# Late expert tiles of a transformer step: 30 whole tiles of 128 rows become 22 whole ones and 5 that two experts share

## The reference

```python
scores = softmax(x @ gate_w.T)                      # 2048 rows, 8 experts
topk_ids, topk_w = _grouped_topk(scores)            # 2 experts for each row, weights sum to 1
gu = jnp.einsum('th,eih->tei', x, w13_weight)       # 256 -> 2 x 512 for each expert
gate, up = (gu[..., :INTER], gu[..., INTER:])
act = jax.nn.silu(gate) * up * combine[:, :, None]
out = jnp.einsum('tei,ehi->th', act, w2_weight)     # 512 -> 256, summed over the two experts
x = x + out
```

## Time and profile before

| | |
|---|---|
| time, median of 3 runs | 571.71 us (571.24 to 571.86) |
| profiled execution, its own time | 574.95 us |
| its span in the profile | 573.1 us |
| PE busy | 539.4 us (94%) |
| DVE, ACT, POOL busy | 298.0, 243.1, 168.7 us |

### The profile page before, as it was taken

One profiled execution on the slowest core, in us unless ns is written; L12 is line 12 of the kernel. 1 busy time (PEld: TensorE's weight loads), 2 busy tenths in 40 slices (PEclk: granted clock), 3 DMA queues, 4 the chain that ended last, 5 costly groups with the idle time before them and its releaser, 6 DMA issues.

```text
span 573.1 us, 11007 instructions
## 1 busy us (share of the span) xinstructions
PE 539.4 (94%) x3932; PEld 443.8 (77%) x3933; DVE 298.0 (52%) x875; ACT 243.1 (42%) x560; POOL 168.7 (29%) x152
## 2 busy tenths in 40 slices
PE   6999999999979999999999689999999999999990
PEld 5888868867555677777776578899999999999990
DVE  6676668989354776847688865671111112111110
ACT  1234755453346676887677434222122221222220
POOL 3120000102043232324130042226443535544432
PEclk9799999999989999999999999999999999999996
DMA  9920000000010000300640944977787888877621
GB/s 328 392 99 2 2 0 2 1 1 5 32 37 1 2 2 1 111 2 1 235 170 7 351 137 149 281 215 236 207 258 223 245 240 224 262 219 254 187 32 22
DMA packets 28507, 74.15 MB, mean 129 GB/s; under 512 B 5584, under 2 KB 20176, under 8 KB 23216
## 3 DMA queue, kind: packets, MB, share of 16 engines
q1 hardware_dynamic: 14368, 57.66, 28.1%
q0 software_dynamic: 7488, 10.39, 9.9%
q10 hardware_dynamic: 6608, 5.54, 3.1%
HBM read 62.86 MB, written 10.72 MB: 128 GB/s over the span
## 4 chain that ended last, share of the span: by engine, by line
PE 65%; DMA 12%; DVE 8%; issue 8%; POOL 2%; DVEq 2%; ACT 1%; POOLq 0%; ACTq 0%
PE ps L858 45%; DMA out_x<-arena,row_no 11%; PE ps L862 9%; PE ps L1150 7%; DVE arena L1506 1%; DVE mx L1644 1%; POOL keep L384 1%; PE ps L1011 1%; PE ps L942 1%; DMA arena<-in_x 1%; PE ps L1002 1%; DVE heads_out L1658 1%; POOL var_x L348 1%; PE ps L985 1%; DVE ring L1843 0%
## 5 line engine op out<-in xcount | busy, mean ns | idle before, releaser
L858 PE MATMUL ps<-keep,arena 128*128 128x128 f32 (+2 forms) x976 | 114.7, 274 | 1.1 <-ACT keep L627 1.1
L858 PEld LDWEIGHTS ps<-keep,arena 128*128 128x128 f32 x976 | 112.6, 192 | 2.6 <-ACT keep L627 1.5
L1953 DVE TENSOR_TENSOR keep<-keep,ps 128x512 f32<-128x512 f32 x39 | 26.8, 688 | 137.0 <-PE ps L858 134.3
L392 POOL DMA_INDIRECT out_x<-arena,row_no x39 | 61.5, 1576 | 108.9 <-DMA out_x<-arena,row_no 65.0
L1150 PE MATMUL ps<-arena,keep 128*128 x312 | 74.0, 381 | 1.2 <-issue 0.9
L356 POOL TENSOR_TENSOR ring<-arena,keep 128x512 f32<-128x512 f32 x32 | 33.4, 1044 | 116.0 <-PE ps L858 98.1
L1150 PEld LDWEIGHTS ps<-arena,keep 128*128 128x128 f32 x312 | 56.4, 191 | 7.8 <-issue 1.9
L587 ACT ACTIVATE ring<-ps,mx 128x128 f32<-128x128 f32 x192 | 52.3, 393 | 13.3 <-DVE mx L1644 13.3
L627 ACT COPY keep<-ps 128x256 f32<-128x256 f32 x39 | 14.5, 371 | 96.8 <-PE ps L862 96.8
L858 PE MATMUL ps<-ring,arena 128*32 128x128 f32 (+1 forms) x640 | 52.9, 348 | 0.5 <-ACT ring L594 0.4
L348 POOL TENSOR_TENSOR var_x<-var_x,minus_half 128x4 f32<-128x4 f32 x16 | 17.0, 1064 | 111.2 <-DVE var_x L1500 111.1
(11 more groups left out here) (259 smaller groups left out, 815.3 us busy)
## 6 DMA issues: line engine op xcount, KB each, us to landing
arena<-in_w SPq DMA_DIRECT2D x29, 1024.0 KB, 5.2
w_first<-in_w SPq DMA_DIRECT2D x10, 1024.0 KB, 5.4
arena<-in_w SPq DMA_DIRECT2D x8, 512.0 KB, 7.2
keep<-in_keep SPq DMA_DIRECT2D x1, 3099.0 KB, 21.1
ring<-in_fold SPq DMA_DIRECT2D x1, 2112.0 KB, 12.4
arena<-in_x SPq DMA_DIRECT2D x4, 512.0 KB, 10.4
arena<-in_ctxT SPq DMA_DIRECT2D x4, 512.0 KB, 7.8
out_x<-arena ACTq DMA_DIRECT2D x4, 512.0 KB, 3.4
```

What stands on the lines that cost most here:

```text
L392: pool.indirect_dma_start(out=out_d, out_offset=bass.IndirectOffsetOnAxis(ap=row_no[:, t:t + 1], axis=0), in_=YO[t % DEEP], in_offset=None ...
L858: ins = pe.matmul(out, w, m, start=(k == 0), stop=(k == len(pairs) - 1))
L1953: dve.tensor_tensor(HA[r % 2], HA[r % 2], ps[:, 2 * (r % 2) + 1, :], ALU.mult).then_inc(act_ok, 1)
```

## The change

Late rows now lie in 22 whole tiles (`FULL`) and 5 shared ones (`SPLIT`), 27 in all, so the program has 36 tiles where it had 39. A shared tile holds 64 rows of one expert in its lower half and 64 of another in its upper half. They stand at tiles 12, 17, 22, 27 and 32 (`SPLIT_AT`). For a shared tile:

- SP loads two experts' weights, so there are 41 loads of 1 MB where there were 39. A buffer is counted in loads (`load(t)`), not in tiles.
- `gate_up_split` turns the product round: 64 rows are stationary, in one column strip of the array for each half, and the weights stream through, 512 columns at a time.
- The products then have rows on partitions, so TensorE transposes them (`turn_products`) and ACT copies them back (`products_turned`). `down_split` does the two halves in column strips again. ACT copies the second expert's `w2` beforehand (`second_down`), and scales in two pieces of 64 partitions.
- `add` issues two DMAs, one behind the other: the first of 64 rows, the second of all 128, whose lower 64 point at holes.

The planning on DVE (`late_tiles`) finds whole tiles and half tiles for each expert, with more stages; `hot_late` covers all 16 batches where it covered 8. The loop over late tiles is written out.

```diff
-NT = B * S * NPICK // P + NE - 1
+HALF = P // 2
...
+HALVES = (B * S * NPICK - EARLY * P + NE * (HALF - 1)) // HALF
+SPLIT = NE // 2 + 1
+FULL = -(-(HALVES - 2 * SPLIT) // 2)
+LATE = FULL + SPLIT
+NT = EARLY + LATE
...
+SPLIT_AT = [EARLY + 3 + 5 * i for i in range(SPLIT)]
...
+def slot(t):
+    if t < EARLY:
+        return t
+    return EARLY + FULL + SPLIT_AT.index(t) if is_split(t) else t - sum(u < t for u in SPLIT_AT)
+def load(t):
+    return t + sum(u < t for u in SPLIT_AT)
...
-                if t >= DEEP:
-                    sp.wait_ge(u_ps, t - DEEP + 1)
-                e = sp.value_load(e_id[0:1, t:t + 1], min_val=0, max_val=NE - 1)
-                sp.dma_start(W13[t % DEEP], w13_d[bass.ds(e, 1), :, :].rearrange("e p n -> (e p) n")).then_inc(w13_in[t % DEEP], 16)
-            sp.wait_ge(added, 16 * NT)
+                for half in range(1 + is_split(t)):
+                    n = load(t) + half
+                    if n >= DEEP:
+                        sp.wait_ge(u_ps, tile_of(n - DEEP) + 1)
+                    col = expert_at(t, half)
+                    e = sp.value_load(e_id[0:1, col:col + 1], min_val=0, max_val=NE - 1)
+                    sp.dma_start(W13[n % DEEP], w13_d[bass.ds(e, 1), :, :].rearrange("e p n -> (e p) n")).then_inc(w13_in[n % DEEP], 16)
+            sp.wait_ge(added, 16 * load(NT))
...
             def add(t):
                 pool.wait_ge(y_ok, t + 1)
-                if t:
-                    pool.wait_ge(added, 16 * t)
-                pool.indirect_dma_start(out=out_d, out_offset=bass.IndirectOffsetOnAxis(ap=row_no[:, t:t + 1], axis=0),
-                                        in_=YO[t % DEEP], in_offset=None, compute_op=ALU.add).then_inc(added, 16)
+                for half in range(1 + is_split(t)):
+                    if t:
+                        pool.wait_ge(added, 16 * (load(t) + half))
+                    own = slice(0, HALF if is_split(t) and not half else P)
+                    rows_at = row_upper[:, SPLIT_AT.index(t):SPLIT_AT.index(t) + 1] if half else row_no[own, slot(t):slot(t) + 1]
+                    pool.indirect_dma_start(out=out_d, out_offset=bass.IndirectOffsetOnAxis(ap=rows_at, axis=0),
+                                            in_=YO[t % DEEP][own, :], in_offset=None, compute_op=ALU.add).then_inc(added, 16)
...
+            def second_down(t):
+                if t == SPLIT_AT[0]:
+                    act.wait_ge(e_known, 2)
+                    act.wait_ge(w2_in, 16 * NE)
+                    act.wait_ge(placed, 2)
+                else:
+                    act.wait_ge(y_ps, SPLIT_AT[SPLIT_AT.index(t) - 1] + 1)
+                col = expert_at(t, 1)
+                at = act.value_load(e_id[0:1, col:col + 1], min_val=0, max_val=NE - 1) * W2_N
+                act.copy(split_w2, w2e[:, bass.ds(at, W2_N)]).then_inc(split_w2_in, 1)
...
+                if is_split(r):
+                    for half, out in enumerate((Y_PS[r % 2], bank(FEED)[:, 0:D])):
+                        own = slice(HALF * half, HALF * half + HALF)
+                        ins = act.activation(YO[r % DEEP][own, :], out[own, :], ACT.Copy, scale=row_w[r % DEEP][own, 0:1])
+                    ins.then_inc(y_ok, 1)
+                    return
...
+            def gate_up_split(t):
+                first, second = W13[load(t) % DEEP], W13[(load(t) + 1) % DEEP]
+                lower, upper = slice(0, HALF), slice(HALF, P)
+                for a, b in ((1, 0), (0, 1)):
+                    for k in range(KD):
+                        at, bt = ((2 * k + g) * INTER for g in (a, b))
+                        one = pe.matmul(ps[lower, 2 * (t % 2) + a, :], XIT[t % 2][:, k, lower], first[:, at:at + INTER], start=(k == 0), stop=(k == KD - 1))
+                        two = pe.matmul(ps[upper, 2 * (t % 2) + b, :], XIT[t % 2][:, k, upper], second[:, bt:bt + INTER], start=(k == 0), stop=(k == KD - 1))
+                one.then_inc(g_ps, 1)
+                two.then_inc(u_ps, 1)
+            def turn_products(t):
+                pe.wait_ge(act_ok, t + 1)
+                if t == SPLIT_AT[0]:
+                    pe.wait_ge(routed, 2)
+                for k in range(INTER // P):
+                    ins = turn(bank(FEED)[:, k * P:(k + 1) * P], split_rows[:, k * P:(k + 1) * P])
+                ins.then_inc(ha_ps, 1)
+            def down_split(t):
+                pe.wait_ge(ha, SPLIT_AT.index(t) + 1)
+                pe.wait_ge(split_w2_in, SPLIT_AT.index(t) + 1)
+                lower, upper, last = slice(0, HALF), slice(HALF, P), INTER // P - 1
+                at = pe.value_load(e_id[0:1, slot(t):slot(t) + 1], min_val=0, max_val=NE - 1) * W2_N
+                for k in range(INTER // P):
+                    pe.matmul(Y_PS[t % 2][lower, :], HA[t % 2][:, k * P:k * P + HALF], w2e[:, bass.ds(at + k * D, D)], start=(k == 0), stop=(k == last))
+                    ins = pe.matmul(bank(FEED)[upper, 0:D], HA[t % 2][:, k * P + HALF:k * P + P], split_w2[:, k * D:k * D + D], start=(k == 0), stop=(k == last))
+                ins.then_inc(y_ps, 1)
...
                 turn_in(m, r + 2)
+                if is_split(r):
+                    turn_products(r)
                 gate_up(m, r + 1)
                 down(m, r)
...
+                beyond = work
+                dve.tensor_tensor(beyond, place, p_len.unsqueeze(1).broadcast_to([P, B, NE]), ALU.is_ge)
...
+                dve.tensor_scalar(base, p_end[:, NE - 1:NE], float(FULL), 2.0, ALU.max, ALU.mult)
+                dve.tensor_scalar(half_end[:, 0:NE], p_end, 2.0, None, ALU.mult)
...
+                done = cmp2[:, 0:(LATE + SPLIT) * 2 * NE].rearrange("p (t n) -> p t n", n=2 * NE)
+                dve.tensor_tensor(done, half_end.unsqueeze(1).broadcast_to([P, LATE + SPLIT, 2 * NE]), kept("half_no").unsqueeze(2).broadcast_to([P, LATE + SPLIT, 2 * NE]), ALU.is_le)
+                dve.tensor_tensor(jump, odd_at, half_end[:, 0:NE], ALU.subtract)
...
-                dve.tensor_tensor(hot_late[k], kept("col_no").unsqueeze(1).broadcast_to([P, EB, P]),
-                                  col_at[:, k * B + EB:(k + 1) * B].unsqueeze(2).broadcast_to([P, EB, P]), ALU.is_equal)
+                dve.tensor_tensor(hot_late[k], kept("col_no").unsqueeze(1).broadcast_to([P, B, P]), col_at[:, of_k].unsqueeze(2).broadcast_to([P, B, P]), ALU.is_equal)```

TensorE's list, first before. This is one late step in the loop: the transposes of tile t+2, `gate_up` of t+1 (`w_first` is the first weight buffer), then the first of the four matmuls of `down`.

```order
L862 MATMUL ps<-keep 128x128 x2
L858 MATMUL ps<-keep,w_first 128x128 x16
L1141 ISA
L1141 TENSOR_LOAD e_id
L1141 ISA x2
L1150 ISA
L1150 MATMUL ps<-arena,keep 128x256
```

More of the change, by code:

```diff
@@ L37, with is_split, tile_of, expert_at @@
 NEG = -3.0e38
+SPLIT_AT = [EARLY + 3 + 5 * i for i in range(SPLIT)]
+def is_split(t):
+    return t in SPLIT_AT
+def slot(t):
[4 more added lines that the diff above has]
+    return t + sum(u < t for u in SPLIT_AT)
+def tile_of(n):
+    return next(t for t in range(NT) if load(t) <= n <= load(t) + is_split(t))
+def expert_at(t, half):
+    return NT + SPLIT_AT.index(t) if half else slot(t)
 def columns(parts):
@@ L184, in build @@
         HOT_N = EB * P // 2
[L185 to L186 removed]
+        hot_early, hot_late = ([ring[:, at + 1024 * k:at + 1024 * k + n * P // 2].bitcast(BF16).rearrange("p (b n) -> p b n", b=n) for k in range(NPICK)]
+                               for at, n in ((512, EB), (512, B)))
         one_hot_early = sb("one_hot_early", [P, NPICK * EB, EARLY], BF16)
@@ L256, in build, with tiles_of @@
         XT_PS, Y_PS = ps[:, 4, 0:D], [ps[:, 5 + u, 0:D] for u in range(2)]
[L258 to L267, removed]
+        UP = 256
+        split_w2, split_rows = ring[:, 0:W2_N], ring[:, W2_N:W2_N + INTER]
+        def tiles_of(step):
+            for t in range(EARLY, NT - 2):
+                step(0, t)
         def bank(k):
@@ L845, in _ @@
             turned(0, 10)
-            tiles_of(act, step)
+            tiles_of(step)
             answer(0, NT - 3)
@@ L1131, in gate_up @@
                 pe.wait_ge(xt, t + 1)
-                pe.wait_ge(w13_in[r % DEEP], 16 * (m + r // DEEP + 1))
+                for n in range(load(t), load(t) + 1 + is_split(t)):
+                    pe.wait_ge(w13_in[n % DEEP], 16 * (n // DEEP + 1))
+                if is_split(t):
+                    gate_up_split(t)
+                    return
+                w13 = W13[load(t) % DEEP]
                 for g, done in enumerate((g_ps, u_ps)):
@@ L1148, in down @@
                     pe.wait_ge(y_ok, t - 1)
+                if is_split(t):
+                    down_split(t)
+                    return
                 for k in range(INTER // P):
@@ L1482, in _ @@
             down(0, 8)
-            tiles_of(pe, step)
+            tiles_of(step)
             gate_up(0, NT - 1)
@@ new lines, in late_tiles @@
+                dve.tensor_scalar(jump, jump, float(HALF), None, ALU.mult)
+                settle()
```

(8 more changed lines are left out.)

91 lines of the change are left out of this document (59 added, 32 removed).

## The result

The changed kernel takes 599.07 us (median of 4 runs, 596.35 to 610.59), the kernel before 571.79 in the same set: a ratio of 1.044 with an interval of 1.039 to 1.049. Runs more than 1.5% above the fastest of the same kernel (here 610.59) count for a median and not for a ratio. The forecast was 582.5 with a range of 565 to 590. The sign came out as written, and so did the line that sets the end; the size did not: +27 us instead of +11, outside the range.

A forecast was written before the change was run, and what follows sets the result against it. Two serial lines, TensorE and the output adds held by weight loads, were taken to matter, the adds setting the end: +11.0 + 2.3 - 2.5 = +10.8 us on 571.71 gives 582.5 us, range 565 to 590.

The forecast's parts named there:

- Which line ends the kernel: Late stage: the adds set the end, falling about 4 us behind TensorE per shared tile; TensorE waits for gathered rows.
- Strips overlap: Split products on TensorE: two column strips run side by side, `gate_up_split` 3.7 to 3.9 us, `down_split` 1.84.
- rival of 588 us by serial strips: Strips don't overlap at 512 columns: 26 us more on TensorE, 588 us; chance 0.05.
- TensorE by itself: TensorE's side: -16.6 for three tiles fewer, +3.8 for shared tiles, +3.1 for planning, -9.7 us in all.
- The shared tile: TensorE's extra time for split products and transposes: 0.75 us for each shared tile, 3.8 for five.
- the planning: Longer `late_tiles` on DVE, in TensorE's path ahead of `down(4)`: +3.1 us with nothing to hide it.
- Start of the line of adds: POOL's late list: `late_rows` ends later, so `fetch(9)`, `add(6)` and all behind it start 2.3 us later.
- The interval beside loads: Late adds: 26 intervals of 5.51 us beside loads and five of 4.54 without, 166.0 against 155.0 us: +11.0.
- pairs of loads hold adds longer: Rival: two loads together hold an add, up to 5.9 us mean interval, 593 us, 588 likelier; chance 0.17.
- Shorter adds of 64 rows: Five adds on POOL have 64 rows and save 0.5 us each: -2.5 us, bounds 0 and -6.

The follow-up runs named there:

- without loads: The changed kernel without the weight loads from load 12 on, late values wrong: 566.66 us, 0.989.
- kernel before without late loads: The kernel before without the weight loads from the twelfth tile on, late values wrong: 571.94 us, 0.998.
- after: The changed kernel itself, with 22 whole and 5 shared late tiles, against the kernel before: 599.07 us, 1.044.
- 27 whole tiles: The changed kernel with all 27 late tiles treated as whole ones, one load and one add each, new planning kept, output wrong: 561.76 us, 0.978.
- one add: The changed kernel with one add for a shared tile instead of two, lower halves of five tiles missing in the output: 575.24 us, 0.997.
- gather first: The changed kernel with the gather for tile t+6 issued ahead of the add of tile t, output complete: 592.72 us, 1.031.
- one load: The changed kernel with one weight load for a shared tile instead of two, five half tiles using the wrong expert: 588.1 us, 1.026.
- pairs apart: The changed kernel with SP waiting longer before loads near a shared tile, so they don't come two at a time, output complete: 590.14 us, 1.031.
- before with quarters: The kernel before with each 1 MB weight load issued as four of 256 KB: 579.39 us, 1.009.

## Why the prediction was right in sign and wrong in size

- **Which line ends the kernel.** Right. TensorE's side is a gain (0.989 without loads), the adds turn it into a loss, and TensorE stands waiting for gathered rows (5.14 us at 444.20, 19.5 in all). It came earlier than forecast, at the first shared tile.
- **Strips overlap.** Right, and fully: 0.43 us a pair. The rival of 588 us by serial strips is out. The Trainium skill's rule in "TensorEngine Tiling (Array Packing)", Tiling Modes, that a mode change drains the engine, shows at most 0.1 us here: the first pair starts 0.31 us behind the start of two transposes whose slot is 0.22.
- **TensorE by itself.** Forecast -9.7, measured 566.66 - 573.9 = -7.2, or -5.3 against the kernel before without late loads (571.94), which is the fairer pair; -16.6 + 5 x 0.95 + 5.3 = -6.5 lies between. The shared tile costs 0.95 instead of 0.75, and the planning 5.3 instead of 3.1: the wait of 3.5 us more was seen (about 3.1), that `down(4)` then runs at half clock was not.
- **Start of the line of adds.** Forecast +2.3. TensorE reached `down(4)` at 372.00 - 0.28 = 371.72 before and at 370.25 - 3.79 = 366.46 after, so add 9 came (410.61 - 366.46) - (409.88 - 371.72) = 6.0 us later, counted from there. That after got there 5.3 us sooner lies within the spread of executions: 27 whole tiles, with the same code up to that point, got there at 371.23 us. From there to add 9 are 43.0 to 44.2 us in the profiled executions of after, one add, gather first, one load and pairs apart, and 38.2 and 37.3 in those of before and before with quarters, so the +6.0 is 5 to 7. The reason is only in part shown: 5.3 us are the planning and the slow `down(4)`; add 4, slowed in its issue (2.82 instead of 1.58 us), stands there too.
- **The interval beside loads.** This is the step that failed most: "26 x 5.51 + 5 x 4.54 = 166.0". 5.51 was TensorE's period, which the adds had only kept up with, and I carried it over to a line that has 6 loads and 6 adds in five tiles. Measured: 5.94, and 26 x 0.43 = 11 us more. What showed in its place is that an add lands just after the last load issued before its own issue is over, so its interval hangs on how the loads lie to it, and four pairs alone made intervals of 9.1, 8.6, 9.4 and 7.9 us. I had this rival ("pairs of loads hold adds longer", 5.9 us, 593) and gave it 0.17. One ground was that the Trainium skill, "DMA: Bandwidth & Descriptors", Queues, rings and completion order, lets a DMA engine change between its queues after each packet. The runs went against what I made of that: an add behind a pair landed after both, 7.1 to 8.7 us.
- **Shorter adds of 64 rows.** Forecast -2.5. The issue is 0.14 us shorter (1.44 against 1.58), but with nothing in the way the next add comes after 3.3 us instead of 4.5: 569.36 to 572.66. Beside loads little of it is seen (431.70 to 438.13, 6.4 us).

The sum closes: +6.0 at the start and +20.4 along the line is +26.4, against +27.3 of the medians. (The two spans differ by 21.1 only: the profiled execution of before is 3.2 us above its median, that of after 2.7 below.) The parts as edits, one on top of the other: whole tiles and planning -12 or -13, split products and pairs of loads +11, second adds +27. They are not independent: taken out of after alone, the pairs are worth 7 to 10 us and the late loads 32.

What stays open: in what order the DMA engines serve the two queues, and why a load itself is late at times. With one load per shared tile an add at 519.10 was still followed by the next only at 528.41, though the loads, at 518.87 and 524.70, were 5.8 us apart. By the completion events the first of these loads took 8.0 us, and the add landed 0.75 us after it.

## What to carry to other kernels

Before counting intervals of a serial line at their present length, find out whether that length is its own or that of what paces it: here 5.51 us was that of TensorE and of its loads. The adds alone take 4.5 us, and more as soon as loads fall onto them. A change that saves tiles of compute but adds links to a line of dependent DMAs and puts transfers back to back beside it can lose more than it saves; a queue that also carries the gathers hands the delay back to compute. Taking one queue's bursts apart helped by 7 to 9 us, cutting them into smaller transfers did not.

## What the runs showed of the hardware that was not expected

- Two float32 strips of 64 columns with 512 moving columns each start 10 ns apart and take one pass time, 0.43 us, for both.
- An accumulating indirect DMA lands after 3.8 us alone, mostly after 4.8 to 6.9 with one 1 MB load of another queue beside it, after 7.1 to 8.7 with two. It lands 0.7 us (median of 16 adds) after the last load that was issued before its own issue was over, even one issued 1.26 us after it began (496.46, 497.72).
- The same 1 MB as four transfers takes more of the engines' time: 3.05 against 2.73 us for each MB in after (12%), 3.07 against 2.89 in the kernel before (7%).
- The issue of one add on POOL took 2.82 us instead of 1.58, at 376.71, while DVE wrote a bf16 mask of 128x2048 (2.28 us from 375.82).
- TensorE's clock stood at its lower level (0.50) for the 6 us behind an idle time of 5.14 us, and was back at 1.00 after that.
